# Ten units of score maxima moved behind the third batch's cross-attention, in a decoder layer with routed experts

## The chip, the cores and the metric

The kernel runs on one core of a Trainium2 chip. Its time is the device time of one execution, in microseconds (us). The engines are TensorE (PE, with its weight loads as PEld), VectorE (DVE), ScalarE (ACT), GpSimd (POOL) and SyncE (SP), which here only issues transfers. Each engine works through its own list in program order and waits on semaphores.

## What is computed

A decoder layer for 4 batches of 256 rows of 128 numbers: causal self-attention with 16 heads, cross-attention with 16 heads of 8 numbers over a context, and a mixture of 8 experts of which each row uses two. Cut to what matters here:

```
x = x + self_attn(layernorm(x))                 # softmax over the query axis
x = x + cross_attn(layernorm(x), ctx)           # 16 heads of 8, softmax over the keys
h = layernorm(x)
scores = h @ Wr + br;  top 2 of 8 experts per row
w = softmax over the two chosen scores
x = x + sum_i  w_i * (relu(h @ W1[i] + b1[i]) @ W2[i] + b2[i])
```

## The kernel before

All order is written out by hand. A list `slots` holds small groups of work items, and each engine walks the same list and does its own part of every item, so the list fixes the order on PE, DVE and ACT. POOL's and SP's lists are written out separately. Batches are numbered 0 to 3, and the last one, 3, is treated by its own rules in the expert stage.

The items that matter here, for a batch b:

- `("MX", b, u)`, 16 units (u from 0 to 15): PE multiplies scores into one PSUM bank (`max_scores`, L974), DVE takes the row maxima of 128 x 512 numbers into `mneg` (`cross_max`, L1565). After unit 15 DVE splits the maxima into three bf16 parts (`split_max`, L1577 to L1580). `("mT", b)` turns them on PE (L983), ACT copies them to `m_part` (L1302), and SP writes them with two transfers into the rows of `q_mem` that the batch's real scores need (`stack_m`, L492). The maxima ride along in the scores' product, so `("CS", b, 0, 0)` waits for these transfers.
- `("CS", b, g, kt)`, 16 per batch: scores on PE (L996), exponential on ACT (`px`, L1315), in banks 0, 1 and 2 in turn. `("CO", b, n)`, 4 per batch: product with the values (L1011), after the exponentials of two groups.
- `oq0, oT0, oq1, oT1, wo` of a batch: its output, a chain that goes PE, DVE, PE, ACT, PE (L1021, L1590 and L1594, L1025, L1328, L1029), then DVE adds the residual and takes statistics (L1555 to L1560), and POOL normalises (`norm_3`, L602 to L649).
- Routing in two parts: `("NT", 0)` and `("RT", 0)` for batches 0 and 1 together, `("NT", 1)` and `("RT", 1)` for batch 2: turned rows (L1041), logits (L1045), the best two on DVE (`best_two`, L1608 to L1627). `("PS", n)` counts the rows ahead of each on PE (`ranks`) and computes their places on DVE (`places`, L1667 to L1689). `("PX", 0)` carries the counts from part 0 to part 1. POOL then scatters the rows to DRAM by `pos_i` (`dispatch`, L691, 12 of them), and SP loads them back in groups as `xr` (L546, three transfers).
- `("WS", 0, i)` and `("W2", 0, i)`: ACT rounds an expert's weights (L1334, L1339); POOL takes the rest of them (`w_lo`, L678, L684). `("XC", n)` copies rows on ACT.
- `("OV", 0)`: DVE finds the experts that overflow (`spares`, L1704 to L1718). `("WU", 0)`: `WARM` idle products on PE (L1111), which compute nothing that is used. Then `("X", 0)`: PE turns the first rows of `xr` (L1104), ACT rounds them (L1352), DVE takes the rest (`x_lo`, L1733), and `("H", 0, 0)` begins the expert products (L822 to L824, L1164 to L1166), which run to the end.

In the order of the list, slots 58 to 65 hold batch 1's scores, 66 to 73 batch 2's and 75 to 82 batch 3's; slot 74 stands between the last two. Slot 83 is batch 3's output, and slot 84 begins the experts.

## Time and profile before

| | |
|---|---|
| median of three runs | 324.31 us (322.19 to 328.33) |
| the profiled execution | 323.46 us, of it 321.4 us span |
| PE busy | 283.1 us, 88% of the span |
| DVE, ACT, POOL busy | 61%, 57%, 46% of the span |
| mean granted TensorE clock | 0.97 of 2.4 GHz |

The span is what the trace shows from the first to the last instruction. Times in the rows are from the span's start; a row's duration can overlap the next one's, because instructions are pipelined. "Idle before" stands in brackets, with the instruction that ended it. A granted clock of 1.00 is 2.4 GHz and 0.50 is 1.2 GHz.

### The profile page before, as it was taken

What the parts mean: (1) busy time and instruction counts of PE and PEld (TensorE: products, weight loads), DVE (VectorE), ACT (ScalarE), POOL (GpSimd) and SP (SyncE); (2) the same over time, 40 slices, a digit from 0 to 9 for tenths busy, and PEclk for the clock granted to TensorE, in tenths of its full rate; (3) what the DMA queues carried; (4) which work ended last, traced back from release to release, by engine and by line L of the source; (5) the groups of instructions that cost most, each with busy time, mean ns of one, the idle gap of its engine ahead of it and who ended that gap; (6) DMA issues with size and microseconds to landing.
All of it is one profiled execution on the core that took longest, in us unless ns stands there. A gap on an engine that the chain in (4) does not pass through costs nothing.

```text
span 321.4 us, 5993 instructions
## 1 busy us (share of the span) xinstructions
PE 283.1 (88%) x2059; PEld 206.4 (64%) x2059; DVE 195.3 (61%) x459; ACT 183.7 (57%) x513; POOL 149.1 (46%) x212
## 2 busy tenths in 40 slices
PE   6889999999989899797999788686689989988985
PEld 2677776877776678454744333432348979988884
DVE  3777566476458885976377484344475675655552
ACT  1769858377737753465277578548206555444331
POOL 7990380127130200720047975437882446544383
PEclk9999999999999999999999799859899999999998
DMA  7900015520590010001067270001182444400301
GB/s 231 216 4 3 4 33 65 67 33 23 153 208 19 20 31 2 5 0 46 6 184 246 73 212 0 4 19 34 53 220 105 174 159 145 148 19 11 100 27 40
DMA packets 27291, 25.24 MB, mean 79 GB/s; under 512 B 3866, under 2 KB 20332, under 8 KB 27260
## 3 DMA queue, kind: packets, MB, share of 16 engines
q1 hardware_dynamic: 24462, 22.46, 26.4%
q0 software_dynamic: 1216, 1.61, 1.7%
q10 hardware_dynamic: 1584, 0.80, 0.9%
q8 instruction: 16, 0.26, 0.3%
q14 instruction: 13, 0.11, 0.1%
HBM read 12.49 MB, written 4.80 MB: 54 GB/s over the span
## 4 chain that ended last, share of the span: by engine, by line
PE 63%; DVE 18%; ACT 5%; issue 5%; POOL 3%; SPq 2%; DMA 2%; ACTq 0%; DVEq 0%; POOLq 0%
PE ps L896 6%; PE ps L822 5%; PE ps L823 5%; PE ps L824 5%; PE ps L929 5%; PE ps L941 4%; PE ps L974 4%; DVE mneg L1565 3%; PE ps L1164 3%; PE ps L1011 3%; PE ps L903 2%; PE ps L1166 2%; PE ps L1165 2%; SPq L484 2%; PE ps L931 2%
## 5 line engine op out<-in xcount | busy, mean ns | idle before, releaser
L1285 ACT ACTIVATE p<-ps,negmax 128x256 f32<-128x256 f32 (+1 forms) x128 | 52.6, 425 | 25.3 <-DVE negmax L1536 25.1
L1565 DVE TENSOR_REDUCE mneg<-ps 128x2 f32<-128x512 f32 x64 | 42.6, 686 | 19.1 <-PE ps L974 19.0
L1315 ACT ACTIVATE px<-ps 128x512 f32<-128x512 f32 x64 | 36.0, 601 | 20.9 <-PE ps L996 20.6
L1536 DVE TENSOR_REDUCE negmax<-ps 128x2 f32<-128x512 f32 (+1 forms) x48 | 33.0, 687 | 19.5 <-PE ps L898 12.4
L1739 DVE SCALAR_TENSOR_TENSOR hid_lo<-ps,hid_hi 128x512 fp32r<-128x512 f32 x42 | 28.6, 690 | 26.5 <-ACT hid_hi L1358 26.5
L1358 ACT ACTIVATE hid_hi<-ps 128x512 fp32r<-128x512 f32 x42 | 25.1, 597 | 31.6 <-PE ps L824 31.4
L709 POOL DMA_INDIRECT ys<-yrow,xr x26 | 25.4, 976 | 27.2 <-DVE yrow L1745 20.6
L602 POOL TENSOR_SCALAR tmp<-mv 128x2 f32<-128x2 f32 x8 | 1.9, 232 | 70.1 <-DVE mv L1560 69.9
L974 PE MATMUL ps<-k_st,q_mem 128*128 128x256 bf16 x128 | 25.4, 282 | 10.0 <-DVE mneg L1565 7.3
L1271 ACT CAST t_hi<-ps 128x512 fp32r<-128x512 f32 x32 | 18.7, 591 | 19.6 <-PE ps L824 18.7
L1285 ACT ACTIVATION_READ_ACCUMULATOR p<-ps,negmax 128x1 f32 x128 | 26.6, 208 | 0.0
L996 PE MATMUL ps<-q_mem,k_st 128*128 128x512 bf16 x64 | 24.8, 413 | 0.5 <-ACT px L1315 0.4
L974 PEld LDWEIGHTS ps<-k_st,q_mem 128*128 128x128 bf16 x128 | 9.3, 99 | 23.3 <-DVE mneg L1565 15.7
L896 PE MATMUL ps<-t_hi,n_parts 128*128 128x512 f32 x64 | 23.1, 442 | 0.2 <-DVE t_lo L1502 0.2
L1164 PE MATMUL ps<-hid_hi,w_hi 128*128 128x256 f32 x64 | 19.3, 302 | 4.2 <-DVE hid_lo L1739 3.8
L1502 DVE TENSOR_TENSOR t_lo<-ps,t_hi 128x512 fp32r<-128x512 f32 x32 | 21.4, 682 | 1.9 <-ACT t_hi L1271 1.8
L822 PE MATMUL ps<-n_parts,g_hi 128*128 128x256 f32 x64 | 20.6, 322 | 0.0
L1011 PE MATMUL ps<-px,v_pad 128*32 128x256 f32 x256 | 18.0, 401 | 2.5 <-ACT px L1315 1.6
L929 PE MATMUL ps<-p,v_sb 128*64 128x256 f32 x128 | 20.1, 392 | 0.0
L822 PE MATMUL ps<-x_hi,w_hi 128*128 128x256 f32 x64 | 18.7, 293 | 1.4 <-issue 1.4
L1166 PE MATMUL ps<-hid_lo,w_hi 128*128 128x256 f32 x64 | 18.0, 282 | 0.0
L823 PE MATMUL ps<-x_hi,w_lo 128*128 128x256 f32 x64 | 18.0, 281 | 0.0
(271 smaller groups left out, 776.8 us busy)
## 6 DMA issues: line engine op xcount, KB each, us to landing
ovw<-w_hi SPq DMA_DIRECT2D x10, 256.0 KB, 2.6
ovw<-w_lo SPq DMA_DIRECT2D x10, 256.0 KB, 2.6
w_raw<-in_L_ffn_W SPq DMA_DIRECT2D x2, 1024.0 KB, 7.7
xs<-pad SPq DMA_DIRECT2D x1, 1716.0 KB, 10.4
k_st<-k_part SPq DMA_DIRECT2D x12, 128.0 KB
q_mem<-q_part SPq DMA_DIRECT2D x48, 32.0 KB
w_last<-in_L_ffn_W SPq DMA_DIRECT2D x4, 256.0 KB, 7.3
w_late<-in_L_ffn_W SPq DMA_DIRECT2D x4, 256.0 KB, 5.2
```

Source lines behind the costliest of these rows:

```text
L822: pe.matmul(out, a[0], b_[0], start=True, stop=False)
L823: pe.matmul(out, a[1], b_[0], start=False, stop=False)
L896: pe.matmul(bank, n_parts[:, a, S * b:S * b + P], t_ring[t][:, 2 * (u % 6):2 * (u % 6) + 2, :], start=(a + t == 0), stop=False)
L929: last = pe.matmul(o, v, p0[:, h, :], start=True, stop=False)
L974: last = pe.matmul(ps[:, max_bank[("MX", b, u)], S * par:S * par + S], q_st[b][:, g, S * par + P * qt:S * par + P * qt + P], k_st[:, g, S ...
L1011: last = pe.matmul(ps[32 * j:32 * j + 32, out_bank(m), S * (g4 % 2):S * (g4 % 2) + S], v_pad[:, TPB * b + kt, (DH + 1) * h:(DH + 1) * h + ...
L1164: pe.matmul(bank, w[0], h[0], start=(opens and n == 0), stop=False)
L1285: last = act.activation(dst, bank[:, n * i:n * i + n], ACT.Exp, bias=negmax[:, kt, h:h + 1], accum_out=psums[:, kt, h:h + 1])
L1315: act.activation(px[:, (g // 2) % 2, c0:c0 + 512], ps[:, score_banks[k], :], ACT.Exp, scale=SCALE_X).then_inc(s_px, 1)
L1536: dve.tensor_reduce(dst, ps[:, k % 3, :].rearrange("p (h q) -> p h q", h=n), AX, ALU.max, negate=True).then_inc(s_max, 1)
L1565: dve.tensor_reduce(mneg[:, qt, :].rearrange("p (r g) -> p r g", r=2)[:, :, g], ps[:, max_bank[("MX", b, u)], :].rearrange("p (h k) -> p h ...
L1739: dve.scalar_tensor_tensor(hid[1][:, n % NC, :], ps[:, hidden_banks[n], :], 0.0, hid[0][:, n % NC, :].bitcast(F32), ALU.max, ALU.subtract) ...
```

## The change

Four things are edited.

1. The last batch's 16 units of maxima move. Before, they stood in slots 63 to 69, one to three in each. Now units 0 to 5 (`MX_BESIDE` = 6) stand one in each of slots 66 to 71, beside batch 2's scores. Units 6 to 15 stand in slot 74, behind batch 2's scores, among batch 2's output items and the routing. They take the banks 0, 1, 2 and 6 in turn in place of 5 and 6.
2. Slot 74 also takes the whole output of batch 2, both steps of the first routing part, the transposition `mT` of batch 3, and logits and choice of the second part; slots 75 to 82 keep only batch 3's scores and values, `PS 1`, its places and one weight rounding. The first logits (`NT 0`, `RT 0`) move from the ends of slots 73 and 74 to those of 72 and 73. `places` becomes an item of its own, `PL`, so that DVE does it later than PE does `ranks`. Weight roundings on ACT are spread anew.
3. `WARM` goes from 24 to 8.
4. In SBUF, `xr` now lies over `w_in` and `q_mem0`, and `hid_hi` and `hid_lo` over `k_st`; before, it was the other way round. No instruction changes by it.

```diff
--- before.py
+++ after.py
@@ -61,7 +61,7 @@
 
 FIRST_OUT = 3
 
-WARM = 24
+WARM = 8
 TWO_ONES = 1.0 + 0x3F80 / 2.0 ** 23
 SCALE_X = float(DH) ** -0.5
 
@@ -96,8 +96,9 @@
             return made
 
 
-        w_in, q_mem0, hid_hi, hid_lo = overlay([("w_in", 4096, F32)], [("q_mem0", 8192, BF16)],
-                                               [("hid_hi", 2048, F32R), ("hid_lo", 2048, F32R)])
+        xr, w_in, q_mem0 = overlay([("xr", 2 * NS * ROW, F32)], [("w_in", 4096, F32)], [("q_mem0", 8192, BF16)])
+        xr = xr[:, :].rearrange("p (n d) -> p n d", d=ROW)
+        k_st, hid_hi, hid_lo = overlay([("k_st", HP * NT * P, BF16)], [("hid_hi", 2048, F32R), ("hid_lo", 2048, F32R)])
         w_nat = w_in[:, 0:3072].rearrange("p (hh c d) -> p hh c d", c=3, d=D)
         wv_c = w_in[:, 3072:4096].rearrange("p (hh d) -> p hh d", d=D)
 
@@ -153,8 +154,6 @@
         negm = sb("negm", [P, 3, NT])
         x_hi, k_part = overlay([("x_hi", 1024, F32R)], [("k_part", 3 * NT * P, BF16)])
         k_part = k_part[:, :].rearrange("p (i n) -> p i n", i=3)
-        xr, k_st = overlay([("xr", 2 * NS * ROW, F32)], [("k_st", HP * NT * P, BF16)])
-        xr = xr[:, :].rearrange("p (n d) -> p n d", d=ROW)
         k_mem = k_st
         k_st = k_st[:, :].rearrange("p (g n) -> p g n", g=HP)
         v_pad = sb("v_pad", [P, NT, (DH + 1) * H + 32])
@@ -278,8 +277,10 @@
 
         MAXIMA = (((2, 5), (1, 1, 1, 2, 2, 1, 1), (3, 0), (1, 1, 2, 2, 1), (3, 5)),
                   ((3, 5), (1, 2, 1, 2, 2, 1, 1), (B, 0), (2, 2, 2), (B, 4)),
-                  ((B, 3), (1, 2, 2, 2, 2), (B + 1, 0), (1, 2, 2, 2), (B + 1, 4)),
-                  ((B + 1, 5), (2, 3, 3), (B + 2, 0), (3, 3, 1, 1), (B + 2, 5)))
+                  ((B, 3), (1, 2, 2, 2, 2), (B + 1, 0), (1, 2, 2, 2), (B + 1, 4)))
+
+        MX_BESIDE = 6
+
 
 
 
@@ -297,6 +298,8 @@
                     max_plan.setdefault((i, s), ([], []))[0].extend(units[:n])
                     units = units[n:]
             max_plan.setdefault(turn, ([], []))[1].append(("mT", b))
+        for u in range(MX_BESIDE):
+            max_plan.setdefault((B + 2, u), ([], []))[0].append(("MX", B - 1, u))
         IN_SLOT = ("V", "T", "n2T", "q", "Z", "PJ")
 
         BESIDE = {
@@ -332,17 +335,19 @@
             units = [("oq0", b - 1), ("oT0", b - 1), ("oq1", b - 1), ("oT1", b - 1), ("wo", b - 1)] if b else \
                 [("V", last, 2), ("V", last, 3), ("Z", last, 2), ("Z", last, 3), ("PJ", last), ("n2T", last), ("q", last)]
             tail = {}
-            for g, unit in zip(((0, 0, 1, 2, 3, 5.5, 6.5), (1.5, 2.5, 3, 4.5, 5.5), (0.5, 1.5, 2, 3, 3.5), (-1, 0, 0.5, 1.5, 2))[b], units):
+            for g, unit in zip(((0, 0, 1, 2, 3, 5.5, 6.5), (1.5, 2.5, 3, 4.5, 5.5), (0.5, 1.5, 2, 3, 3.5), ())[b], units):
                 tail.setdefault(g, []).append(unit)
             more = {(1, 4): [("WS", 0, 0)], (1, 5): [("WS", 0, 1)], (1, 6): [("WS", 0, 2)],
                     (1, 7): [("WS", 0, 3), ("BT", 0)], (2, 0): [("WS", 0, 4)], (2, 1): [("WS", 0, 5)],
-                    (2, 2): [("WS", 0, 6)], (2, 3): [("WS", 0, 7)], (2, 4): [("XC", 0)], (2, 5): [("W2", 0, 0)],
-                    (2, 7): [("W2", 0, 1), ("NT", 0)], (3, 0): [("XC", 1), ("PS", 0)], (3, 1): [("W2", 0, 2)],
-                    (3, 2): [("PX", 0)], (3, 3): [("W2", 0, 3)], (3, 4): [("NT", 1)], (3, 5): [("RT", 1), ("XC", 2)],
-                    (3, 6): [("W2", 0, 4)], (3, 6.5): [("PS", 1)]}
+                    (2, 4): [("WS", 0, 6), ("XC", 0)], (2, 6): [("NT", 0), ("WS", 0, 7)], (2, 7): [("RT", 0), ("W2", 0, 0)],
+                    (3, 0): [("PS", 1)], (3, 0.5): [("PL", 1)], (3, 3): [("W2", 0, 4)]}
             if b == last:
 
-                slots.append([("CO", b - 1, 3), ("RT", 0), ("oq0", b - 1)])
+                rest = [("MX", b, u) for u in range(MX_BESIDE, 2 * HP)]
+                slots.append(rest[0:1] + [("CO", b - 1, 3)] + rest[1:3] + [("PS", 0), ("XC", 1), ("oq0", b - 1)] + rest[3:4] +
+                             [("oT0", b - 1), ("W2", 0, 1), ("oq1", b - 1)] + rest[4:5] + [("oT1", b - 1), ("PL", 0),
+                              ("W2", 0, 2), ("wo", b - 1)] + rest[5:] + [("W2", 0, 3), ("mT", b), ("PX", 0), ("NT", 1), ("XC", 2),
+                              ("RT", 1)])
             for g in range(HP):
                 maxima_now, turn = max_plan.get((B + b, g), ([], []))
                 slot = [("CS", b, g, 0)] + tail.get(g - 0.5, []) + more.get((b, g - 0.5), []) + maxima_now[:1] + [("CS", b, g, 1)]
@@ -417,8 +422,11 @@
             if key[0] == "MX":
                 n = len(max_bank)
                 bank = 6 if at < z_all or n % 2 == 0 else 5
+                if key[1] == B - 1 and key[2] >= MX_BESIDE:
+                    bank = (0, 1, 2, 6)[(key[2] - MX_BESIDE) % 4]
                 max_bank[key], max_before[key], in_bank[bank] = bank, in_bank.get(bank, 0), n + 1
         first_in_5 = next(k for k in max_bank if max_bank[k] == 5)
+        all_in_5 = in_bank[5]
 
         XR_PARTS = ((0, 2), (2, 6), (6, NS))
         N1T_OUT = 6
@@ -969,9 +977,12 @@
                         pe.wait_ge(s_vx_ev, 1)
                 if ("MX", b, u) == first_in_5:
                     pe.wait_ge(s_z_ev, 4 * B)
+                bank = max_bank["MX", b, u]
+                if bank < 3 and max_before["MX", b, u] == 0:
+                    pe.wait_ge(s_px, last_in(bank, enumerate(score_banks[:2 * HP * (B - 1)])) + 1)
                 ge(pe, s_mx_ev, max_before[("MX", b, u)])
                 for par in range(2):
-                    last = pe.matmul(ps[:, max_bank[("MX", b, u)], S * par:S * par + S],
+                    last = pe.matmul(ps[:, bank, S * par:S * par + S],
                                      q_st[b][:, g, S * par + P * qt:S * par + P * qt + P],
                                      k_st[:, g, S * b:S * b + S], start=True, stop=True)
                 last.then_inc(s_mx, 1)
@@ -1066,7 +1077,7 @@
                 one = hots[g]
                 n = one.shape[1] - 1
                 if g == 0:
-                    pe.wait_ge(s_mx_ev, 16 * B)
+                    pe.wait_ge(s_mx_ev, all_in_5)
                 else:
                     pe.wait_ge(s_rank_ev, g)
                 pe.wait_ge(s_tab, 9)
@@ -1784,7 +1795,7 @@
                         gates()
                     elif kind == "GS":
                         two_gates(b)
-                    elif kind == "PS":
+                    elif kind == "PL":
                         places(b)
                     elif kind == "PX":
                         carry()
```

The lists of POOL and SP are the same before and after. What the table of slots does shows in the order of the instructions. On DVE, from the end of the choice of part 0 (L1627 before, L1638 now), with `mneg` the maxima, `r_den` and `o_n` batch 2's output, `over` and what follows it the places. Before:

```order
L1627 TENSOR_TENSOR gate<-top 128x4
L1590 RECIPROCAL r_den<-ps 128x16
L1594 TENSOR_TENSOR o_n<-ps,r_den 128x64 x2
L1667 TENSOR_SCALAR over<-ps 128x8
L1670 TENSOR_TENSOR prod<-lower,over 128x64
L1671 TENSOR_REDUCE rank<-prod 128x8
```

and now:

```order
L1638 TENSOR_TENSOR gate<-top 128x4
L1576 TENSOR_REDUCE mneg<-ps 128x2 x3
L1601 RECIPROCAL r_den<-ps 128x16
L1605 TENSOR_TENSOR o_n<-ps,r_den 128x64 x2
L1576 TENSOR_REDUCE mneg<-ps 128x2
L1601 RECIPROCAL r_den<-ps 128x16
L1605 TENSOR_TENSOR o_n<-ps,r_den 128x64 x2
L1576 TENSOR_REDUCE mneg<-ps 128x2
L1678 TENSOR_SCALAR over<-ps 128x8
L1681 TENSOR_TENSOR prod<-lower,over 128x64
```

Five of the ten units stand here between the choice and the places. A little further on DVE, from `pos_i`, the last instruction of the places, to `base`, the first of the carry. Before:

```order
L1689 TENSOR_SCALAR pos_i<-slot_f 128x8
L1590 RECIPROCAL r_den<-ps 128x16
L1594 TENSOR_TENSOR o_n<-ps,r_den 128x64 x2
L1555 TENSOR_TENSOR resid<-ps,resid 128x256
L1559 BN_STATS stats<-resid 128x6
L1560 BN_AGGR mv<-stats 128x2
L1559 BN_STATS stats<-resid 128x6
L1560 BN_AGGR mv<-stats 128x2
L1695 TENSOR_TENSOR base<-over,shift 128x8
```

and now:

```order
L1700 TENSOR_SCALAR pos_i<-slot_f 128x8
L1566 TENSOR_TENSOR resid<-ps,resid 128x256
L1570 BN_STATS stats<-resid 128x6
L1571 BN_AGGR mv<-stats 128x2
L1570 BN_STATS stats<-resid 128x6
L1571 BN_AGGR mv<-stats 128x2
L1576 TENSOR_REDUCE mneg<-ps 128x2 x5
L1588 CAST m_split<-mneg 128x4x8
L1589 TENSOR_TENSOR m_rest<-mneg,m_split 128x32
L1590 CAST m_split<-m_rest 128x4x8
L1591 TENSOR_TENSOR m_split<-m_rest,m_split 128x4x8
L1706 TENSOR_TENSOR base<-over,shift 128x8
```

The other five units and the split of the maxima stand here, in front of the carry. On PE, from batch 2's last output product (`wx`, `oT`) on, with `hot` and `below` of the second part's ranks. Before:

```order
L1029 MATMUL ps<-wx,oT 128x128 x2
L996 MATMUL ps<-q_mem,k_st 128x512 x4
L1011 MATMUL ps<-px,v_pad 32x256 x8
L1041 MATMUL ps<-ident,xrow 128x128 x2
L996 MATMUL ps<-q_mem,k_st 128x512 x2
L1045 MATMUL ps<-wr_sb,nT 128x8 x2
L996 MATMUL ps<-q_mem,k_st 128x512 x2
L1011 MATMUL ps<-px,v_pad 32x256 x8
L996 MATMUL ps<-q_mem,k_st 128x512
L1075 MATMUL ps<-hot,below 128x40
```

and now:

```order
L1040 MATMUL ps<-wx,oT 128x128 x2
L985 MATMUL ps<-k_st,q_mem 128x256 x10
L994 MATMUL ps<-ident_b,m_split 48x128 x2
L1052 MATMUL ps<-ident,xrow 128x128 x2
L1056 MATMUL ps<-wr_sb,nT 128x8 x2
L1007 MATMUL ps<-q_mem,k_st 128x512 x2
L1086 MATMUL ps<-hot,below 128x40
```

Batch 2's output product was followed by scores of batch 3 (`ps<-q_mem,k_st` 128x512). Now ten products for maxima (five units), the turned maxima, the rows and the logits of part 1 come first, and batch 3's first two scores stand behind them.

## Rows read from the trace of the kernel before

**Rows 1.** windows, three stretches: busy us of each engine, granted clock, DMA share, GB/s

```profile
186.99:203.68 16.69, 14.40 (x135) 6.64 (x132) 8.82 (x25) 14.31 (x31) 12.12 (x17) 1.00 0.23 64
226.10:230.99 4.89, 1.94 (x11) 1.11 (x11) 1.61 (x8) 1.69 (x5) 3.67 (x5) 0.97 0.17 53
230.99:234.10 3.11, 3.11 (x9) 1.71 (x10) 1.75 (x6) 0.46 (x1) 3.08 (x4) 0.50 0.13 32
```

**Rows 2.** timeline, PE, 180 to 241: start us, duration us, operation, idle before

```profile
180.00 0.61 PE L974 MATMUL ps<-k_st,q_mem 128*128 128x256 bf16 x2 [2.09 <-DMA q_mem<-q_part]
...
186.99 0.38 PE L996 MATMUL ps<-q_mem,k_st 128*128 128x512 bf16 x1
...
213.22 1.94 PE L1011 MATMUL ps<-px,v_pad 128*32 128x256 f32 x16
...
220.37 0.41 PE L1041 MATMUL ps<-ident,xrow 128*128 128x128 f32 x2 [1.38 <-POOL xrow L649]
...
224.99 1.07 PE L1011 MATMUL ps<-px,v_pad 128*32 128x256 f32 x16 [0.94 <-ACT px L1315]
...
230.99 1.23 PE L1029 MATMUL ps<-wx,oT 128*128 128x128 f32 x4 [0.35 <-ACT oT L1328]
232.01 6.41 PE L1111 MATMUL ps<-mask,ident_b 128*128 128x512 bf16 x24
...
240.30 0.36 PE L822 MATMUL ps<-x_hi,w_hi 128*128 128x256 f32 x1 [1.45 <-issue]
```

**Rows 3.** timeline, SyncE's queue, 176 to 243: start us, us issuing, transfer

```profile
179.43 1.56 SPq L492 DMA_DIRECT2D q_mem<-m_part  x2
...
200.20 1.60 SPq L492 DMA_DIRECT2D q_mem<-m_part  x2
```

**Rows 4.** windows, the stretch in which the last data of the second m_part transfer move

```profile
202.60:202.80 0.20, 0.12 (x4) 0.13 (x8) 0.00 (x0) 0.20 (x2) 0.20 (x1) 1.00 0.07 18
```

**Rows 5.** the chain, 177.62: start us, us, what

```profile
177.62 2.33 DMA q_mem<-q_part
```

**Rows 6.** timeline, ACT, 199 to 203

```profile
199.81 0.36 ACT L1302 CAST m_part<-ps 48x256 bf16<-48x256 f32 x1
...
200.58 2.04 ACT L1315 ACTIVATE px<-ps 128x512 f32<-128x512 f32 x4
```

**Rows 7.** timeline, DVE, 184 to 239

```profile
184.07 4.32 DVE L1565 TENSOR_REDUCE mneg<-ps 128x2 f32<-128x512 f32 x7
...
195.91 0.18 DVE L1577 CAST m_split<-mneg 128x32 bf16<-128x32 f32 x1
...
196.56 0.19 DVE L1580 TENSOR_TENSOR m_split<-m_rest,m_split 128x32 bf16<-128x32 f32 x1
...
204.77 0.19 DVE L1608 COPY score<-ps 128x32 f32<-128x32 f32 x1 [6.59 <-PE ps L1045]
...
207.34 0.16 DVE L1627 TENSOR_TENSOR gate<-top 128x4 f32<-128x4 f32 x1
...
208.94 0.17 DVE L1667 TENSOR_SCALAR over<-ps 128x8 f32<-128x8 f32 x1 [0.89 <-PE ps L1080]
...
211.61 0.17 DVE L1689 TENSOR_SCALAR pos_i<-slot_f 128x8 uint32<-128x8 f32 x1
...
216.35 0.42 DVE L1555 TENSOR_TENSOR resid<-ps,resid 128x256 f32<-128x256 f32 x1 [4.02 <-PE ps L1029]
...
233.53 3.05 DVE L1704 TENSOR_TENSOR rank<-rank,taken 128x8 f32<-128x8 f32 x1
...
238.73 0.20 DVE L1718 TENSOR_REDUCE b2col<-spare 128x5 f32<-128x40 f32 x1
```

**Rows 8.** timeline, POOL, 217 to 237

```profile
217.81 0.24 POOL L602 TENSOR_SCALAR tmp<-mv 128x2 f32<-128x2 f32 x1 [1.39 <-DVE mv L1560]
...
231.62 4.92 POOL L684 TENSOR_TENSOR w_lo<-w_raw,w_hi 128x512 fp32r<-128x512 f32 x4
```

**Rows 9.** DMA issues, 170 to 245: transfer, queue, count, KB, median us to landing

```profile
xr<-xs SPq DMA_DIRECT2D x1, 264.0 KB, 3.0
```


## Prediction

> **What bounds the kernel now.** I read the windows first. While batch 2's scores run, from 186.99 to 203.68, PE is busy 14.40 of 16.69 us and ACT 14.31, and DVE, which has the maxima, only 8.82: no engine is far from full and DVE has room [rows 1]. Then I followed PE's timeline for its waits. At 180.00 it had stood 2.09 us, because the first unit of batch 3's maxima waits for that batch's `q_mem` transfers, and all later work of PE is queued behind it [rows 2]. Batch 2's first score starts at 186.99, batch 3's last values product ends at 224.99 + 1.07 = 226.06, its output product at 230.99 + 1.23 = 232.22. Then come 24 idle products of 6.41 us, and the expert products begin at 240.30 [rows 2]. From there on PE has its own work to the end, which the change doesn't touch. So the question is by how much the first expert product moves. The working below walks one path: batch 2's first score, first logits, DVE's list behind them, batch 3's first score, its last values, its output, the experts. Times are on the profiled execution's own scale.
>
> **Batch 2's scores begin sooner.** Without maxima in slots 63 to 65 nothing on PE waits for the transfer of 180.00. The next wait is for batch 2's own maxima, which SP finishes issuing at 179.43 + 1.56 = 180.99 [rows 3]. When they land has no row of its own. Lower bound: the same pair for batch 3 was issued by 200.20 + 1.60 = 201.80 [rows 3], and its last data moved before 202.80 [rows 4], so at least 1.0 us. Upper bound: 2.33 us, the landing of a `q_mem` transfer on the chain [rows 5]. So 182.0 to 183.3. ACT has six exponentials and three weight roundings to do from about 178.4; at 2.04 / 4 = 0.51 us each [rows 6] that ends at 183.0. I take 183.1 for the first score, 3.9 sooner than 186.99.
> The Trainium skill ("DMA: Bandwidth & Descriptors", "Anatomy of one DMA") puts a transfer's fixed cost at about 2.0 us; as an estimate by that page the maxima would land at 183.0, inside the bounds, and no run here separates its parts.
>
> **The first logits.** Before, from batch 2's first score to the copy of the logits took 204.77 - 186.99 = 17.8 us [rows 2, 7]. The new stretch holds six units in place of eight and two roundings (the last `WS` and one `W2`) fewer or later; at the old pace it ends at 200.9. Both PE and ACT were near full there [rows 1], so two units and a rounding less can give back 1 to 1.5 us, but the normalised rows of batch 1 come no earlier, since on POOL `norm_3` stands behind the rest of weight 6, whose rounding moved to slot 70. I take 200.0, 4.8 sooner than before (199 to 201).
>
> **What now stands behind them on DVE.** Before, the work behind the logits overlapped batch 3's scores. Now those scores wait for maxima that DVE has yet to take. DVE's list, each part from its rows [rows 7]:
> - the choice: 204.77 to 207.34 + 0.16, 2.7 us, to 202.7
> - three maxima at 4.32 / 7 = 0.62 us: 1.85, to 204.6
> - batch 2's first normalisation, 0.6 us (207.50 to 208.94, of it 0.89 idle): 205.2, then one maximum to 205.8
> - the second normalisation, which comes back through PE, ACT and PE: 0.6 us and a wait that no single row shows, an estimate between 0 and 2 us; I take 1.1: to 207.5, then one maximum to 208.1
> - the places: 208.94 to 211.61 + 0.17, 2.84 us, to 210.9
> - residual and statistics: 216.35 to 217.71 (POOL starts on them at 217.81 [rows 8]), 1.36 us, to 212.3
> - five maxima: 3.1, to 215.4, and the split, 195.80 to 196.75, 0.85 us, to 216.25.
>
> PE's part of the maxima, 0.61 us or less a pair, hides beside DVE. Then the turn on PE and the copy of 0.36 us on ACT [rows 6]: 217.0. SP issues two transfers in 1.60 us [rows 3]: 218.6. They land 1.0 to 2.3 us later by the bounds above; I take 2.0, near the row that is a landing: **batch 3's first score at 220.6**. The other branch is earlier: from the end of the places to the rows of part 1 on PE took 220.37 - 211.78 = 8.6 us, of it 1.39 in which POOL waited for batch 2's statistics [rows 2, 8]. From 210.9 without that wait it is 218.1, and its logits 0.7 us later stand in front of the score but hold nothing up.
>
> **Batch 3's scores.** They have no output steps between them now. ACT is the limit: 16 exponentials at 0.51 = 8.2 us, one `W2` and one copy of values, about 1 us [rows 6]. On PE every second slot has a values product of 1.07 us [rows 2], whose wait for exponentials leaves ACT idle some 0.3 us each time, 1.0 in all, and the last values product adds 1.07: 11.2 us in sum. To this comes the clock. PE does little between 201 and 220.6. Before, it had thin stretches too while batch 2's output ran through DVE, and the values product at 213.22 took 1.94 us against 1.07 at full clock [rows 2]. So the first scores and perhaps one such product run at 1.2 GHz; bounds 0 and 2.5 us, I take 0.9, one slow product. The last values end at 220.6 + 11.2 + 0.9 = 232.7.
>
> **Batch 3's output** is untouched: 232.22 - 226.06 = 6.16 us [rows 2], to 238.9.
>
> **The end of the idle products.** Before, first expert product minus end of output was 240.30 - 232.22 = 8.1 us. PE's branch: 24 products took 6.41 us, and the clock was 0.50 until 234.10 [rows 1, 2]. Eight products are then five at half clock and three at full, 0.43 and 0.22 us, 2.8 us; the step from idle products to experts stays 240.30 - 238.42 = 1.9 us. Sum 4.7. DVE's branch: `spares` stand in front of `x_lo`. Their first instruction took 3.05 us, from 233.53 to 236.58 [rows 7], and POOL's run of `w_lo` ended at 231.62 + 4.92 = 236.54 [rows 8]; its like take 0.20. POOL now scatters sooner and has that run behind it by about 236, before the output ends, so 2.85 us of the stall go: 1.3 + 2.5 for statistics and spares, 0.8 for `x_lo`: 4.6. Both branches say 4.7, so 3.4 us are gained.
> A page explains the stall: the Trainium skill ("SBUF — State Buffer", "SBUF: two separate sides") says that an instruction of VectorE with two SBUF inputs and one of GpSimd that reads SBUF exclude each other for their whole length. By that rule it would come back if the runs met again, 2.85 us.
> The rows `xr` don't bind: the second part's places come by 225.5 and 12 scatters end by about 231, the first `xr` transfer lands 3.0 us after issue [rows 9], at 235. The cut of the idle products alone, before, could have saved little: PE could have turned rows at 235.9, yet DVE's spares ended only at 238.93 [rows 7]. The new overlay in SBUF costs nothing: no instruction goes with it, and it only lets `xr` land while `k_st` is read.
>
> **Sum.** 238.9 + 4.7 = 243.6 against 240.30: 3.3 us later. Signed parts: -4.8 at the logits, +11.5 between logits and last values (32.7 against 21.3), -3.4 behind the output. The profiled execution took 323.46 us, 0.85 below the median; on the median 324.31 + 3.3 = **327.6 us**.
>
> **Rivals.**
> *The other side, faster:* the transfers. If the pair of maxima lands 1.0 us after issue, as the data rows allow [rows 4], at both places, batch 2's first score is bound by ACT alone and batch 3's comes at 219.6; if the logits then come at 199.0 and the clock costs nothing, the sum is 3.3 - 1.0 - 1.0 - 0.9 = +0.4, and with the second normalisation's wait (1.1) filled by its neighbour, -0.7: 323.6 us. The point that decides is batch 3's first score at 217.5 with a full clock. For it: no row shows a landing of these small transfers. Against: DVE's list alone is 15 us, and all its durations are measured. Chance 0.2.
> *The clock stays low:* PE is thin from 201 on, the output chain of batch 3 is thin too (1.94 of 4.89 us, after which the clock was 0.50 [rows 1]), and the clock may not have risen when 8 products are done. Then batch 3's scores lose 2.5 us instead of 0.9 and the first expert products run at 1.2 GHz for some 3 us, 1.5 lost: 3.3 + 1.6 + 1.5 = +6.4, 330.7 us. Chance 0.17. The Trainium skill ("TensorE: Matmul & The Clock Gate", "What's actually happening") holds a low clock to be the default that only activity lifts, which speaks against this change as a whole; by that rule this rival is the result, while here the clock did hold through the pause of 1.45 us ahead of 240.30 [rows 2].
> *It doesn't do what it says:* the logits are not sooner than 202, because batch 1's rows wait on POOL for the moved rounding. +5.3, 329.6 us. Chance 0.13.
> *Forecast*, with its own range of 325 to 330: chance 0.5.
>
> **Range and chances.** The measurement tells 2%, 6.5 us, from no change. Range 323 to 331.5: from the fast rival's neighbourhood to just past the slow ones. Faster by over 2% (below 317.8) has no case of its own, 0.03. Slower by over 2% (above 330.8) is half the clock rival and the tail of the others, 0.14. Within 2%: 0.83.
>
> **What would show it.** Right: no wait of PE near 180; batch 2's first score near 183; logits copied near 200; ten maxima on DVE between 202.7 and 215.4; a gap on PE before batch 3's first score near 220.6 that ends with a `q_mem` transfer; the last values near 232.7; no instruction of 3 us among the spares; first expert product near 243.6. Wrong: batch 3's first score before 218, its scores in under 10 us, or a first expert product that waits for `xr`.

## The result and the profile after

The changed kernel takes **330.91 us** (median of 4 runs, 329.06 to 331.30); the kernel before took 324.47 (322.19 to 328.33) in the same comparison. The ratio is 1.021, with a 95% interval of 1.014 to 1.028: slower beyond the noise, while the interval leaves open whether by more or less than 2%. Some executions of a kernel are over a per cent longer, at a lower granted clock, and all ratios here leave them out. The forecast was 327.6 us in a range of 323.0 to 331.5: slower, as forecast, and inside the range, but 3.3 us above the forecast.

First the timeline of PE after the change, from batch 2's first score to the first expert product. Source lines are higher by 11 than before: L1007 are the scores, L1022 the values products, L985 the maxima, L994 their turn, L1052 and L1056 keys and logits, L1040 the output product, L1122 the idle products.

```profile
179.08 0.29 PE L994 MATMUL ps<-ident_b,m_split 128*48 128x128 bf16 x2 [0.34 <-DVE o_n L1605]
...
184.70 0.39 PE L1007 MATMUL ps<-q_mem,k_st 128*128 128x512 bf16 x1 [1.13 <-DMA q_mem<-m_part]
...
199.84 0.63 PE L1052 MATMUL ps<-ident,xrow 128*128 128x128 f32 x4 [1.52 <-POOL xrow L657]
...
201.14 1.79 PE L1056 MATMUL ps<-wr_sb,nT 128*128 128x8 f32 x8 [0.24 <-ACT nT L1398]
...
211.57 1.91 PE L985 MATMUL ps<-k_st,q_mem 128*128 128x256 bf16 x8
215.51 0.61 PE L985 MATMUL ps<-k_st,q_mem 128*128 128x256 bf16 x2 [2.02 <-DVE mneg L1576]
219.04 0.38 PE L994 MATMUL ps<-ident_b,m_split 128*48 128x128 bf16 x2 [2.92 <-DVE m_split L1591]
220.85 0.66 PE L1052 MATMUL ps<-ident,xrow 128*128 128x128 f32 x2 [1.44 <-POOL xrow L657]
221.97 1.02 PE L1056 MATMUL ps<-wr_sb,nT 128*128 128x8 f32 x4 [0.46 <-ACT nT L1398]
223.33 0.63 PE L1007 MATMUL ps<-q_mem,k_st 128*128 128x512 bf16 x1 [0.34 <-issue]
...
226.83 1.90 PE L1022 MATMUL ps<-px,v_pad 128*32 128x256 f32 x16
...
235.76 1.07 PE L1022 MATMUL ps<-px,v_pad 128*32 128x256 f32 x16 [0.96 <-ACT px L1326]
...
241.76 0.82 PE L1040 MATMUL ps<-wx,oT 128*128 128x128 f32 x4 [0.35 <-ACT oT L1339]
242.81 3.08 PE L1122 MATMUL ps<-mask,ident_b 128*128 128x512 bf16 x7 [0.22 <-issue]
...
247.77 0.36 PE L830 MATMUL ps<-x_hi,w_hi 128*128 128x256 f32 x1 [1.45 <-issue]
```

Read it against [rows 2]. The wait of 2.09 us at 180.00 is gone. Between the logits (201.14 to 202.93) and batch 3's first score (223.33) there are now 20 us in which PE does maxima, output steps and routing, with waits of 2.02 and 2.92 us for DVE. The first values product after them took 1.90 us, the last 1.07.

The same stretches as windows show which engine is busy in them, and at which clock (DVE is the third pair of numbers, the granted clock stands ahead of the last two).

```profile
184.70:202.97 18.27, 14.22 (x118) 7.76 (x120) 6.34 (x17) 13.37 (x29) 14.77 (x19) 0.95 0.42 116
202.97:223.33 20.36, 11.63 (x67) 6.60 (x67) 15.10 (x63) 4.15 (x11) 9.86 (x12) 0.58 0.05 16
223.33:236.83 13.50, 10.34 (x84) 3.14 (x84) 3.65 (x21) 9.26 (x18) 10.43 (x10) 0.81 0.23 66
```

In the middle one DVE is busy 15.10 of 20.36 us and ACT only 4.15: ACT's exponentials, which filled [rows 1]'s first stretch, have nothing to work on. The granted clock is 0.58 on the mean there.

DVE's timeline of that stretch, to hold against [rows 7]:

```profile
202.97 0.19 DVE L1619 COPY score<-ps 128x32 f32<-128x32 f32 x1 [6.97 <-PE ps L1056]
...
205.61 1.88 DVE L1576 TENSOR_REDUCE mneg<-ps 128x2 f32<-128x512 f32 x3
...
209.61 0.26 DVE L1601 RECIPROCAL r_den<-ps 128x16 f32<-128x16 f32 x1 [0.84 <-PE ps L1032]
...
213.43 0.17 DVE L1700 TENSOR_SCALAR pos_i<-slot_f 128x8 uint32<-128x8 f32 x1
...
214.79 3.05 DVE L1576 TENSOR_REDUCE mneg<-ps 128x2 f32<-128x512 f32 x5
...
218.70 0.19 DVE L1591 TENSOR_TENSOR m_split<-m_rest,m_split 128x32 bf16<-128x32 f32 x1
```

The starts of two executions can't be compared directly. The turn of batch 2's maxima stands ahead of everything that the change touches, apart from where buffers lie, and it comes at 179.08 here and at 176.83 in the trace of before. In the 14 profiles of this study it lies between 176.83 and 179.22, in no order with the kernel. I therefore measure from it. From that turn to the first expert product took 68.69 us after and 63.47 before: **5.2 us more**. Behind it the spans have 81.1 us left in both. This is one pair of executions, and the origin does not remove all of their scatter: the first experiment below has the order of the kernel before and took 61.04 us for the same path.

### The profile page after: what moved, and what is told of

Read it like the earlier page. It is cut to its first block, busy times and chain, and to the rows that moved or that the text cites. A ratio compares the mean times of both kernels' runs of the same rounds, so it can differ in the third digit from the quotient of the medians.

```text
span 328.9 us, 5943 instructions
## 1 busy us (share of the span) xinstructions
PE 280.9 (85%) x2025; PEld 206.3 (63%) x2043; DVE 193.5 (59%) x459; ACT 183.3 (56%) x513; POOL 148.8 (45%) x212
## 4 chain that ended last, share of the span: by engine, by line
PE 64%; DVE 17%; issue 6%; ACT 5%; POOL 3%; DMA 3%; SPq 0%; another core or an unknown queue 0%; ACTq 0%; DVEq 0%; POOLq 0%
PE ps L904 6%; PE ps L830 5%; PE ps L831 5%; PE ps L832 5%; PE ps L937 5%; PE ps L949 4%; PE ps L1022 4%; PE ps L985 4%; PE ps L1175 3%; DVE mneg L1576 3%; PE ps L1177 2%; PE ps L1176 2%; PE ps L911 2%; DMA w_in<-in_L_attn_W_qkv 2%; PE ps L939 2%
## 5 line engine op out<-in xcount | busy, mean ns | idle before, releaser
L717 POOL DMA_INDIRECT ys<-yrow,xr x26 | 25.4, 977 | 27.2 <-DVE yrow L1756 21.3
L985 PE MATMUL ps<-k_st,q_mem 128*128 128x256 bf16 x128 | 26.1, 295 | 9.7 <-DVE mneg L1576 8.7
L1007 PE MATMUL ps<-q_mem,k_st 128*128 128x512 bf16 x56 | 20.5, 402 | 3.7 <-ACT px L1326 2.2
L985 PEld LDWEIGHTS ps<-k_st,q_mem 128*128 128x128 bf16 x128 | 10.5, 104 | 20.5 <-DVE mneg L1576 14.4
L830 PE MATMUL ps<-n_parts,g_hi 128*128 128x256 f32 x64 | 20.6, 321 | 0.0
L1022 PE MATMUL ps<-px,v_pad 128*32 128x256 f32 x256 | 18.8, 416 | 2.0 <-ACT px L1326 1.0
```

Of the source, the lines that this page charges most:

```text
L830: pe.matmul(out, a[0], b_[0], start=True, stop=False)
L985: last = pe.matmul(ps[:, bank, S * par:S * par + S], q_st[b][:, g, S * par + P * qt:S * par + P * qt + P], k_st[:, g, S * b:S * b + S], st ...
L1022: last = pe.matmul(ps[32 * j:32 * j + 32, out_bank(m), S * (g4 % 2):S * (g4 % 2) + S], v_pad[:, TPB * b + kt, (DH + 1) * h:(DH + 1) * h + ...
```

## The experiments

Each is the kernel before or after with one edit; the diffs are cut to the lines that carry it. They were timed in three groups on three chips (the first four kernels, the next four, the last four), each group beside the kernel before, so a difference between kernels of two groups is safer read from the ratios than from the medians. First three that go with parts of the change one at a time.

**The buffers alone.** The kernel before with the change's `overlay` lines, nothing else.

```diff
-w_in, q_mem0, hid_hi, hid_lo = overlay([("w_in", 4096, F32)], [("q_mem0", 8192, BF16)],
-                                       [("hid_hi", 2048, F32R), ("hid_lo", 2048, F32R)])
+xr, w_in, q_mem0 = overlay([("xr", 2 * NS * ROW, F32)], [("w_in", 4096, F32)], [("q_mem0", 8192, BF16)])
+k_st, hid_hi, hid_lo = overlay([("k_st", HP * NT * P, BF16)], [("hid_hi", 2048, F32R), ("hid_lo", 2048, F32R)])
-xr, k_st = overlay([("xr", 2 * NS * ROW, F32)], [("k_st", HP * NT * P, BF16)])
```

> The kernel before with the new overlay in SBUF alone. In the trace of the changed kernel everything stood 2.25 us later already before the first moved instruction, from the landing of w_in at the start (6.8 us). If that is chance of one execution, this kernel is within 1 us of the kernel before. If the overlay did it, it is 2 to 2.5 us slower and its first encoded heads (t_lo) come near 18 us.

Measured: 324.77 us over 10 runs, ratio 1.000 (0.996 to 1.003). The placement costs and gives nothing; with it alone the turn of batch 2's maxima came at 179.22 and the time did not move. This trace is also a second one of the order of the kernel before:

```profile
182.36 0.39 PE L973 MATMUL ps<-k_st,q_mem 128*128 128x256 bf16 x2 [2.06 <-DMA q_mem<-q_part]
...
188.11 0.38 PE L995 MATMUL ps<-q_mem,k_st 128*128 128x512 bf16 x1
...
205.90 0.19 DVE L1607 COPY score<-ps 128x32 f32<-128x32 f32 x1 [6.60 <-PE ps L1044]
...
240.26 0.36 PE L821 MATMUL ps<-x_hi,w_hi 128*128 128x256 f32 x1 [1.45 <-issue]
```

From the turn to batch 2's first score it took 8.89 us where the profile of before has 10.16, to the copy of the logits 26.68 for 27.94, to the first expert product 61.04 for 63.47. (Behind that it has 82.5 us left where the others have 81.1, so to the end of the span it is 1.0 us shorter.) The wait for `q_part` is in both. Behind it the granted clock was 1.00 here (182.30 to 188.30) and 0.75 there (180.00 to 186.00); from 200 to 224 it was 0.93 and 0.79. So the same order of work differs by 2.4 us of this path between two executions, along with the clock.

**The idle products alone**, in either kernel:

```diff
-WARM = 24
+WARM = 8
```

> The kernel before with 8 idle products in place of 24. Main theory: DVE's spares hold the first expert product, so at most 0.6 us is gained (-0.6 to 0). Rival (idle products are pure delay): the rows had landed near 235.9, so 2 us are gained. Rival (clock): the experts begin at 1.2 GHz, 1.5 to 3 us are lost.

Measured: 323.53 us over 10 runs, ratio 0.998 (0.994 to 1.001). Sixteen products fewer are not seen in the time. Two things in the trace show why. First DVE's timeline, the first instruction of the spares (L1704), then the first expert product on PE:

```profile
237.00 2.60 DVE L1704 TENSOR_TENSOR rank<-rank,taken 128x8 f32<-128x8 f32 x1
239.63 0.20 DVE L1706 TENSOR_TENSOR spare<-spare_no,rank 128x40 f32<-128x40 f32 x1
```

```profile
242.63 0.55 PE L822 MATMUL ps<-x_hi,w_hi 128*128 128x256 f32 x1 [3.00 <-issue]
```

2.60 us for an instruction whose likes take 0.20, the row of [rows 7] again, and `x_lo` follows the spares without a pause. So with eight idle products the spares hold the experts, as the prediction had it. The experts then come 6.95 us behind the output product instead of 8.08, but after 3.00 us of standing they begin at half clock: the granted clock was 0.50 for the first 2 us and 0.76 for the next 2.4, and the span has 82.0 us left behind their start instead of 81.1. The gain of 1.1 us and the loss of 0.9 nearly cancel.

> The changed kernel with 24 idle products again. Main theory: the cut from 24 to 8 gained about 3.5 us there, since the spares no longer stall, so this is 3 to 3.7 us slower than the changed kernel, 334 us. Rival (the few idle products leave the experts at 1.2 GHz): it is no slower than the changed kernel.

Measured: 333.35 us (ratio 1.027, 1.023 to 1.031), 2.4 us above the kernel after. The last output product ended at 240.99 and the first expert product came at 249.74, 8.75 us later; with eight idle products it was 247.77 - 242.58 = 5.19. So in the kernel after the cut is worth 2.4 us timed (the runs of the two kernels don't overlap), 3.6 in the traces. What the profiles give and what the runs give differ by a microsecond more than once below; for verdicts I go by the runs.

**All sixteen units beside batch 2's scores.** If the ten displaced units of maxima are the loss, doing none of them behind the scores must win it back.

```diff
-        MX_BESIDE = 6
+        MX_BESIDE = 16
-            max_plan.setdefault((B + 2, u), ([], []))[0].append(("MX", B - 1, u))
+            max_plan.setdefault((B + 2, u // 2), ([], []))[0].append(("MX", B - 1, u))
```

> The changed kernel with all 16 units of maxima beside batch 2's scores, two in each of its eight slots; slot 74 has none. Main theory (ten reductions in series in front of batch 3's scores cost 6.2 us, but the logits of part 1 hold those scores too, until about 3 us earlier than now): 2 to 3 us faster than the changed kernel if batch 2's slots lose nothing; they lose 0 to 2, so 328 to 331 us. Rival (the maxima alone are the loss): 5 to 6 us faster, 325 us. Rival (the clock is the loss): no change.

Measured: 331.20 us, ratio 1.021: no change at all, just outside the 328 to 331 of the main theory. The theory "the maxima alone are the loss" fell. PE's timeline of this kernel shows what took their place:

```profile
213.17 0.41 PE L994 MATMUL ps<-ident_b,m_split 128*48 128x128 bf16 x2 [1.03 <-DVE resid L1566]
...
220.03 0.66 PE L1052 MATMUL ps<-ident,xrow 128*128 128x128 f32 x2 [6.46 <-POOL xrow L657]
```

Counted from batch 2's turn of the maxima, batch 3's comes 3.9 us sooner (213.17 - 177.08 against 219.04 - 179.08), and PE then stands 6.46 us for part 1's keys, which are written ahead of batch 3's first score and wait for POOL's three scatters and its norm. Batch 3's first score came at 222.03, 44.95 us behind that turn, where it was 44.25 in the kernel after.

**Part 1's keys back beside batch 3's scores**, on that kernel and on the kernel after (lines shortened to the items that move):

```diff
-("mT", b), ("PX", 0), ("NT", 1), ("XC", 2), ("RT", 1)])
+("mT", b), ("PX", 0)])
-(3, 0): [("PS", 1)], (3, 0.5): [("PL", 1)], (3, 3): [("W2", 0, 4)]}
+(3, 3): [("W2", 0, 4)], (3, 4): [("NT", 1)], (3, 5): [("RT", 1), ("XC", 2)],
+(3, 6): [("PS", 1)], (3, 6.5): [("PL", 1)]}
```

> The kernel after with all sixteen of the last batch's units of maxima beside batch 2's scores (as in e4_all_beside), and with part 1's keys and logits (NT 1, RT 1) and its ranks and places put back beside batch 3's scores, where the kernel before has them. Theory now: in the kernel after two lists end just ahead of batch 3's first score, each long enough by itself, the maxima with their transfer (to about 223 us) and part 1's keys, which wait for POOL (to about 222 us); with both gone the score waits for the transfer of the maxima alone, which in e4_all_beside could start at 213.6 us: score at about 218 us, first expert product at about 241 to 242 us, time 323.5 us (322.5 to 325.5), some 7 us under e4_all_beside. Rival, the low clock that batch 3's scores inherit from the thin stretch ahead is the loss, whatever stands in it: less than 3 us under e4_all_beside, 328.5 us or more.

Measured: 329.29 us, ratio 1.015 (1.010 to 1.020). Batch 3's first score came where expected, the gain did not; the time is the rival's (328.5 or more). PE's timeline:

```profile
213.67 0.41 PE L994 MATMUL ps<-ident_b,m_split 128*48 128x128 bf16 x2 [1.03 <-DVE resid L1566]
218.02 2.48 PE L1007 MATMUL ps<-q_mem,k_st 128*128 128x512 bf16 x5 [3.94 <-DMA q_mem<-m_part]
...
236.22 1.22 PE L1040 MATMUL ps<-wx,oT 128*128 128x128 f32 x4 [0.35 <-ACT oT L1339]
...
244.51 0.55 PE L830 MATMUL ps<-x_hi,w_hi 128*128 128x256 f32 x1 [3.01 <-issue]
```

The score at 218.02 waits for the maxima's transfer and for nothing else. But from the last output product (ended 237.44) to the experts are 7.07 us where the kernel after has 5.19. DVE's and POOL's timelines there:

```profile
238.75 2.72 DVE L1715 TENSOR_TENSOR rank<-rank,taken 128x8 f32<-128x8 f32 x1
```

```profile
236.51 4.93 POOL L692 TENSOR_TENSOR w_lo<-w_raw,w_hi 128x512 fp32r<-128x512 f32 x4
```

With part 1 routed later, POOL scatters until 236.49 and has its four roundings behind that; the spares meet them, and end with them: 238.75 + 2.72 = 241.47 against 236.51 + 4.93 = 241.44. And after the 3.01 us for which PE stands there, the experts begin slow: the granted clock was 0.50 from 244.51 to 249.00, and the span has 83.0 us left behind their start, 1.9 more than in the kernel after. So the early routing of part 1 is not only a loss: it clears POOL and takes away the stall of 3.05 us of [rows 7]. In the five kernels with part 1 routed early that instruction took 0.13 us, in all others 1.81 to 3.56.

> The kernel after with only part 1's keys, logits, ranks and places put back beside batch 3's scores; the ten units of maxima stay behind batch 2's scores. Theory of two lists: the transfer of the maxima still holds batch 3's first score until about 222.5 us, the keys and logits then cost their own 1 to 1.5 us among the scores, so no change that can be told: 331 us (330 to 332). Rival, part 1's keys alone are the loss and the maxima cost nothing: 327 us or less.

Measured: 331.10 us, ratio 1.022: no change, as expected. In its trace the turn of the maxima is at 217.19 and batch 3's first score at 221.50, 4.31 us later, and 44.42 us behind batch 2's turn (44.25 in the kernel after). Two lists end just ahead of batch 3's first score, and taking either away leaves the other. The stall is back here too, 1.81 us.

**The wait at 180 alone.** The kernel before, with the last batch's maxima begun behind batch 2's first score:

```diff
-                  ((B + 1, 5), (2, 3, 3), (B + 2, 0), (3, 3, 1, 1), (B + 2, 5)))
+                  ((B + 2, 0), (3, 3, 3, 3), (B + 2, 4), (2, 2), (B + 2, 6)))
```

> The kernel before with one change: the last batch's maxima begin behind batch 2's first score instead of in the middle of batch 1's, all sixteen done beside batch 2's scores, their turn one slot later. It takes away the wait of 2.09 us for the queries of batch 3 (at 180.00 us) and adds no list between batches 2 and 3. Theory: the wait was on the path, so about 1.5 to 2 us sooner, 322.6 us (321.8 to 323.6), batch 2's first score near 184.9 us and the logits' copy near 202.7 us. Rival, VectorE is then late with sixteen reductions in batch 2's scores and gives the gain back: 324.5 us or more.

Measured: 324.71 us over 10 runs, 324.15 over the seven that the ratio uses, ratio 1.007 (1.001 to 1.013). The wait did go and batch 2's first score came at 182.94, yet no time was won; the theory fell, and the rival's 324.5 is near. PE's timeline at the end of batch 2, then DVE's, and POOL's:

```profile
200.69 0.38 PE L983 MATMUL ps<-ident_b,m_split 128*48 128x128 bf16 x2 [2.44 <-DVE m_split L1580]
```

```profile
195.06 2.45 DVE L1565 TENSOR_REDUCE mneg<-ps 128x2 f32<-128x512 f32 x4
197.62 1.25 DVE L1577 CAST m_split<-mneg 128x32 bf16<-128x32 f32 x1
198.90 1.20 DVE L1578 TENSOR_TENSOR m_rest<-mneg,m_split 128x32 f32<-128x32 f32 x1
```

```profile
197.56 1.27 POOL L678 TENSOR_TENSOR w_lo<-w_raw,w_hi 128x512 fp32r<-128x512 f32 x1
198.79 1.26 POOL L684 TENSOR_TENSOR w_lo<-w_raw,w_hi 128x512 fp32r<-128x512 f32 x1
```

PE now waits 2.44 us for DVE's split of the maxima, two of whose instructions took 1.25 and 1.20 us in place of 0.19. They lie on POOL's two roundings, 197.56 to 198.83 and 198.79 to 200.05, and each ends within 0.05 us of one. This is what the Trainium skill ("SBUF — State Buffer", "SBUF: two separate sides") describes: VectorE and GpSimd share a pair of ports, the first to start has it for its whole instruction, and VectorE takes it for an operation with two SBUF inputs (where GpSimd's instruction reads SBUF, as these roundings do) or in a two-port mode. The second of the two instructions has two SBUF inputs; the first is a cast with one, for which the page's other case would have to hold. Counted from the turn of batch 2's maxima the logits are copied after 28.00 us, against 27.94 before and 26.68 with the new placement. Eight reductions that stood ahead of batch 2's first score now stand beside its scores. VectorE is not full there (14.90 of 22.38 us), but its last four reductions and the stalled split are what PE waits for at the end.

**The clock.** The kernel after with 17 unread products of 128x512 in its waits (`WF n` stands for n of them):

```diff
-rest[5:] + [("W2", 0, 3), ("mT", b), ("PX", 0), ("NT", 1), ("XC", 2), ("RT", 1)])
+rest[5:9] + [("WF", 4)] + rest[9:] + [("WF", 7), ("W2", 0, 3), ("mT", b),
+ ("WF", 4), ("PX", 0), ("NT", 1), ("WF", 2), ("XC", 2), ("RT", 1)])
```

> The kernel after with 17 products of 128x512 whose result nobody reads put where TensorE waits between batches 2 and 3: four ahead of the last unit of maxima, seven behind it, four behind the turn of the maxima, two behind part 1's keys. They change no list and fill only waits. Theory: the waits are the loss and the low clock (0.50 from 212 to 228 us) adds about 2 us to it, in batch 3's first scores and the output: granted clock back at 1.00 before batch 3's first score, 329 us (328 to 330). Rival, the clock is the whole loss: 326 us or less. Rival, the products lie in the way and give nothing: 331 us or more.

Measured: 328.40 us, ratio 1.013 (1.007 to 1.018), 2.5 us under the kernel after. The windows of its list and of batch 3's scores:

```profile
200.27:220.36 20.09, 12.74 (x84) 6.63 (x83) 15.51 (x63) 4.87 (x12) 10.20 (x13) 0.92 0.05 16
220.36:232.38 12.02, 8.95 (x85) 2.98 (x86) 3.35 (x20) 9.26 (x18) 9.86 (x11) 1.00 0.14 46
```

The mean clock was 0.92 and 1.00 in place of 0.58 and 0.81, and the scores took 12.02 us in place of 13.50. The list ahead of them got only 0.27 us shorter, 20.09 for 20.36, since DVE has most of it. Together 1.75 us. A further 0.72 us of the traces' difference lies ahead of the first unread product, in the logits (1.06 us here, 1.79 in the profile of after), where the two programs are the same: a chance of the two executions. So the low clock costs 1.75 us by the traces and 2.5 by the medians, which come from two chips and whose ratios have intervals that overlap.

**The clock in the two other kernels.** Fifteen such products in three waits of the kernel before, twenty-eight in three of the kernel with all maxima beside and part 1 back:

```diff
+        for key, n, ranked in ((("oT0", 2), 6, 0), (("oT1", 2), 5, 1), (("NT", 1), 4, 1)):
+        for key, n, ranked in ((("PS", 0), 10, 0), (("mT", 3), 4, 1), (("CS", 3, 0, 0), 14, 1)):
+            slot = next(s for s in slots if key in s)
+            slot.insert(slot.index(key), ("WF", n, ranked))
```

> The kernel before with 15 products of 128x512 whose result nobody reads, put where TensorE waits for another engine among batch 3's scores: six ahead of the turn of the first output rows (wait 2.01 us at 208.11), five ahead of that of the second (1.33 us at 212.39), four ahead of part 1's keys (1.38 us at 220.37). Theory: the low clock around 213 to 218 us costs the kernel before about as much as its slow rows are over their twins at full clock (0.87 us in the 16 products at 213.22, 0.4 in the output product, 0.5 in the scores behind), so 322.7 us, 1.5 us less. Rival: those products hide behind ScalarE's exponents or VectorE, and the time is the same within 0.5 us, 324.2 us.

Measured: 323.85 us over 11 runs, ratio 0.998 (0.994 to 1.001). The clock was 1.00 from 200 to 224 where it had been 0.79; counted from the turn of batch 2's maxima the trace is 1.75 us shorter (321.7 - 178.88 = 142.82 against 321.4 - 176.83 = 144.57), but the runs show no gain outside their interval. The comparison with that one trace misleads: the kernel with the new placement, with no such products and a clock of 0.93 there, took 61.04 us from the turn to the experts, this one 61.61. No gain that can be told, as the rival had it.

> The kernel e5_beside_back with 28 unread products of 128x512 in its waits between batches 2 and 3: ten ahead of the counts of part 0 (wait 3.20 us), four ahead of the turn of the maxima (1.03 us), fourteen ahead of batch 3's first score (3.94 us). Theory: the low clock is worth there what e8_after_busy gave back (2 to 2.5 us): 327 us (326 to 328), which leaves some 2.5 us over the kernel before for the output, the choice and the transfer of the maxima standing in a row instead of beside scores. Rival: nothing else is lost than the clock, 324.5 us or less.

Measured: 327.61 us over 10 runs, ratio 1.009 (1.005 to 1.013): 1.7 us under the same kernel without them, as expected (326 to 328), and still 3.5 us above the kernel before. Its experts too began below full clock, 0.78 for the first 2 us and 0.57 for the next 3.

**The ten units left out**, in both kernels. In the kernel after `rest` is empty; in the kernel before the last row of `MAXIMA` has the first six units alone (the waits that count the units are adjusted, not shown):

```diff
-                rest = [("MX", b, u) for u in range(MX_BESIDE, 2 * HP)]
+                rest = []
-                  ((B + 1, 5), (2, 3, 3), (B + 2, 0), (3, 3, 1, 1), (B + 2, 5)))
+                  ((B + 1, 5), (2, 3, 1), (B + 2, 0), (), (B + 2, 5)))
```

> The kernel after without its ten units of maxima behind batch 2's scores: products and reductions are left out, batch 3's scores subtract batch 2's maxima in their place. Theory: VectorE's list then ends at part 0's places and the residual, the turn of the maxima follows the output, transfer from there: batch 3's first score 5 to 6 us sooner but held by part 1's keys, which wait for POOL, so 3 to 4 us off the time, 327.5 us. Rival, the maxima are the whole loss: 7 us or more off, 324 us or less.

> The kernel before without the same ten units of the last batch's maxima (units 6 to 15, which it has beside the scores of batches 1 and 2); batch 3's scores subtract batch 2's maxima in their place. Theory from e7_before_late_max: VectorE's list sets batch 2's pace, so ten reductions of 0.62 to 0.69 us less bring the logits about 4 us sooner, and the time falls by 3 to 4 us, 320.5 us: then the ten cost the same wherever they stand, and the kernel after has to carry them plus what stands in a row. Rival, they are hidden beside the scores: 323.5 us or more, and moving them could win nothing.

Measured: 328.70 us (ratio 1.011, 1.005 to 1.017) from the kernel after, 322.35 over 10 runs (ratio 0.996, 0.992 to 0.999) from the kernel before. The first is 1.2 us above its theory (327.5), and its rival fell; the second lies between its theory (320.5) and its rival (323.5 or more). Without any of the ten in either, the changed order is still 328.70 - 322.35 = 6.4 us slower; with them the difference is 330.91 - 324.47 = 6.4. The equality is partly luck: by the ratios, each taken against its own runs of the kernel before, it is 1.5% without the ten (4.9 us) and 2.1% with them (6.8 us), each give or take 2.3 us. So the ten cost 2.2 to 3.4 us where the change puts them and 1.4 to 2.1 where they were, and most of the loss stays without them. PE's timeline of the kernel after without them:

```profile
211.47 0.41 PE L994 MATMUL ps<-ident_b,m_split 128*48 128x128 bf16 x2 [1.03 <-DVE resid L1566]
218.33 0.66 PE L1052 MATMUL ps<-ident,xrow 128*128 128x128 f32 x2 [6.45 <-POOL xrow L657]
...
220.33 1.01 PE L1007 MATMUL ps<-q_mem,k_st 128*128 128x512 bf16 x2
```

and of the kernel before without them:

```profile
201.37 1.06 PE L1045 MATMUL ps<-wr_sb,nT 128*128 128x8 f32 x8
...
203.20 0.59 PE L996 MATMUL ps<-q_mem,k_st 128*128 128x512 bf16 x2
```

There batch 3's scores follow the logits product within 1 us; here they stand 19 us behind it.

## Why the prediction was right, and where it was short

Its mechanism held in the main: batch 3's scores lose their cover and start behind a row of output, choice, places, maxima and transfer. Two waits that it put at nothing, both of part 1's routing, turned up in the same stretch. Counted from the turn of batch 2's maxima, step by step:

- **Batch 2's first score**: forecast 3.9 us sooner, measured 4.5 (184.70 - 179.08 = 5.62 against 186.99 - 176.83 = 10.16). Against the trace with the new placement (8.89) it is 3.3. The transfer's wait that I could not see before is 1.13 us, its end 1.4 us after SP had issued (181.66 + 1.56 = 183.22), 2.17 on the chain, between my bounds of 1.0 and 2.3.
- **The first logits**: forecast 4.8 sooner, measured 4.05 (2.8 against the trace with the new placement). The 0.75 us that are missing are the logits product's own: it ran at half clock, 1.79 us for 1.06, after PE had stood 1.52 us for POOL's rows, which were queued behind two roundings. That queue is the mechanism of the rival "not sooner than 202", and this profile did copy them at 202.97 - 2.25 = 200.7 on the scale of before; so the rival did not come true, though its wait is there.
- **Logits to batch 3's first score**: forecast 20.6 us, measured 20.36. The choice and the places came as listed, and DVE's list from the logits to the split took 15.92 us (218.89 - 202.97) for the 16.25 assumed, with 0.84 of the 1.1 for the second normalisation's wait. The branch that I had put aside, part 1's keys and logits, was the one that ended last, by the row: their product ended at 222.99 and the score followed at 223.33, without the transfer as its releaser, which I had named as a sign. On the scale of before the branch ended at 220.7 and not at 218.8: its rows came 0.5 us later, and its logits ran at half clock (1.02 us for 0.61) behind a wait of 0.46. The transfer ended close to it: in the kernels whose score did wait for the transfer, the score came 4.31 to 4.35 us behind the turn of the maxima (3.81 and 4.11 with the waits filled), which from 219.04 is 222.9 to 223.4.
- **Batch 3's scores**: forecast 12.1 us, measured 13.50. **This is the term that failed most**, in two parts. I had priced the clock at one slow values product, 0.9 us. It stayed at 0.50 until 228, through the first six scores and the first values product, and with the clock up the same stretch took 12.02, so it cost 1.5. The other 11.2 were 12.02 even at full clock. Of the 0.8 between them the greater part is a wait that I had put nowhere: the third score stands behind `PS 1`, whose products wait for DVE's choice of part 1.

```profile
224.85 0.19 PE L1086 MATMUL ps<-hot,below 128*128 128x40 bf16 x1 [0.88 <-DVE hot L1631]
```

With the waits filled it was still 0.56 us.

- **Output**: forecast 6.16, measured 5.75.
- **End of the idle products to the experts**: forecast 4.7, measured 5.19. There was no stall in the spares, as forecast, and the eight idle products ran at half clock, 3.08 us for seven that the trace shows.

The missed parts are +0.75 - 0.24 + 1.40 - 0.41 + 0.49 = 2.0, which takes the forecast 3.3 to the 5.2 that the traces show (0.1 is rounding). The rest of the 6.4 us between the medians, 1.2 us, is of the size by which traces of the order of before differ: against the one with the new placement the kernel after is 7.7 us longer to the experts, 6.2 to the end of the span. So this part of the miss need not be in the forecast's terms; it can come from the one trace that it started from.

Two slips in the recorded sums change nothing: the signed part between logits and last values is 32.7 - 21.3 = 11.4, not 11.5, and the split of the maxima began at 195.91, not 195.80, which makes it 0.84 us.

Of the rivals, the low clock (330.7 us) came nearest in time, and nearer than the forecast, but only part of its mechanism is there: the scores lost 1.5 us to the clock where it had 2.5, and filling the waits gave back 1.75 to 2.5 in all. Its other half, experts at a low clock, did not happen in this kernel; they ran at full clock from 247.77. It did happen where the stall held them, at 242.63 and 244.51 in the two kernels above. The faster rival was refuted at its own point: batch 3's first score, on the scale of before, came at 223.33 - 2.25 = 221.1, not 217.5.

After the experiments the loss reads so. It is 6.4 us by the medians whether or not the ten maxima are done, 6.8 and 4.9 by the ratios, so the rest of the order is enough to cause most of it: output, choice and places of batch 2 no longer beside batch 3's scores, and part 1's keys ahead of them. This does not show the ten to be free: without them part 1's keys hold the first score (6.45 us of waiting), and without those the transfer of the maxima does. How it divides between these two no run shows; the kernel with all maxima beside and part 1 back was 5.0 us over the kernel before, with the waits filled 3.5, but there the transfer of the maxima and the spares had become waits instead, and the experts began below full clock. Of the 6.4, some 2 us (1.75 by the traces, 2.5 by the runs) are the low clock that such a thin row brings. The cut of the idle products pays 2.4 us of it back; in the kernel before, where part 1 is routed late and the spares stall, it gave nothing that can be told. What is sooner in front, 3 to 4 us at the logits, is real but was bought with work that DVE must do later.

No kernel here that does all the maxima beats the kernel before by more than its interval. The two that came nearest, 323.53 us with eight idle products and 323.85 with the filled waits, both have intervals that reach beyond 1.

## What to carry to other kernels

Before a wait for a transfer is taken away, ask which engine used it for its list, and where that list goes: here a wait of 2 us, removed by itself, came back as 2.4 us of waiting for VectorE. To learn whether a moved piece is the cause of a loss, leave it out of both kernels; if most of the difference stays, as here, the rest of the order is enough to cause it. When several lists end at the same point, removing one shows nothing, so an experiment without effect clears nobody until the other list is gone as well. And look at a second trace of the same order before a difference of 2 us is placed: here the kernel before alone spans 2.4 us on the path in question.
